# Two-layer graph network on one core: the stage between the layers rewritten, its tables made elsewhere

## The reference, cut to what matters

```python
h = relu(layernorm(x))
# layer 0: an edge network gives a 16x16 matrix per edge
w = (relu(ea16 @ W1 + b1) @ W2 + b2).reshape(E, 16, 16)
out = segment_sum(einsum('ei,eio->eo', h[src], w), dst) + h @ root + bias
out = (out - out.mean(0)) / sqrt(out.var(0) + eps) * gamma + beta      # batch norm
x = x + relu(out)
h = relu(layernorm(x))
# layer 1: tensor product of h[dst] with 8 edge features, summed at src
m = silu(einsum('ei,ej,ijh->eh', h[dst], ea8, W_msg_tp) * c) @ W_msg_lin * c2
agg = segment_sum(m, src)
x = (x + h) + silu(einsum('ni,nh,ihk->nk', h, agg, W_upd_tp) * c3) @ W_upd_lin * c2
```

## Time and profile before

| | us |
|---|---|
| median of 3 runs (lowest, highest) | 7573.94 (7566.49, 7576.72) |
| the profiled execution | 7580.85 |
| its span | 7579.1 |

### The profile page before, as it was taken

How to read it: one execution, slowest core, us unless ns; L and a number is a source line. 1 busy time by engine, 2 the same in 40 slices (tenths; PEclk the granted TensorE clock), 3 DMA queues, 4 the chain that set the end, 5 groups by cost and what they waited for, 6 DMA issues and landing times. The chain is left out here.

```text
span 7579.1 us, 190087 instructions
## 1 busy us (share of the span) xinstructions
PE 6892.4 (91%) x52101; PEld 5979.1 (79%) x52101; DVE 6492.7 (86%) x16891; ACT 4377.7 (58%) x8232; POOL 5712.3 (75%) x4880
## 2 busy tenths in 40 slices
PE   6999999999999999999997699999999999999984
PEld 4777777777777777777776599999999999999981
DVE  6888888888888888888888899999999999999985
ACT  3444444444444444444443577777777777777760
POOL 5777777777777777777776388888888888888880
PEclk9999999999999999999999899999999999999997
DMA  2111111111111111111111454444555555545442
GB/s 53 20 20 20 19 20 20 20 20 20 20 20 20 19 20 20 20 20 20 20 20 33 99 73 73 72 72 71 73 74 71 73 72 72 73 72 74 72 57 39
DMA packets 699525, 333.83 MB, mean 44 GB/s; under 512 B 422354, under 2 KB 643920, under 8 KB 699498
## 3 DMA queue, kind: packets, MB, share of 16 engines
q0 software_dynamic: 336128, 66.50, 15.4%
q1 hardware_dynamic: 362188, 263.59, 13.8%
q10 hardware_dynamic: 1182, 3.44, 0.1%
HBM read 300.69 MB, written 32.35 MB: 44 GB/s over the span
## 5 line engine op out<-in xcount | busy, mean ns | idle before, releaser
L695 POOL DMA_INDIRECT xg<-gather_rows,idx x3232 | 3069.1, 950 | 998.7 <-issue 980.3
L1445 POOL DMA_INDIRECT sums<-total,row x1616 | 2617.9, 1620 | 535.5 <-issue 410.0
L805 PE MATMUL ps_w<-W2s,hT 128*128 128x256 f32 x12928 | 2977.4, 383 | 46.2 <-DVE prod L869 43.4
L805 PEld LDWEIGHTS ps_w<-W2s,hT 128*128 128x128 f32 x12928 | 2431.7, 190 | 562.1 <-DVE prod L869 201.0
L1416 PE MATMUL ps_wide<-hot_col,placed 128*128 128x392 f32 x12928 | 2437.4, 346 | 20.2 <-ACT hot_col L1358 11.4
L1416 PEld LDWEIGHTS ps_wide<-hot_col,placed 128*128 128x128 f32 x12928 | 2317.0, 196 | 51.4 <-issue 39.0
L869 DVE TENSOR_TENSOR prod<-ps_w,xg 128x512 f32<-128x512 f32 x1616 | 1079.6, 689 | 502.3 <-DMA xg<-gather_rows,idx 338.9
L734 ACT ACTIVATE hT<-ps_h,b1c 128x512 f32<-128x512 f32 x1616 | 1018.0, 680 | 312.9 <-PE ps_h L793 312.0
L1257 DVE SCALAR_TENSOR_TENSOR placed<-iota,src_r,halves 128x512 fp32r<-128x512 bf16 x1616 | 1103.1, 744 | 0.1
L1352 ACT ACTIVATE square<-iota_col,minus_col 128x784 bf16<-128x784 int16 x1212 | 1056.4, 934 | 17.0 <-PE ps_wide L1416 17.0
L876 DVE TENSOR_REDUCE msg<-prod 128x32 f32<-128x512 f32 x1616 | 1058.6, 676 | 0.0
(11 more groups left out here) (185 smaller groups left out, 4995.7 us busy)
## 6 DMA issues: line engine op xcount, KB each, us to landing
dst_row<-dst_rows SPq DMA_DIRECT2D x404, 256.0 KB
xg<-gather_rows,idx POOLq DMA_INDIRECT x3232, 2.4
src_row<-src_rows SPq DMA_DIRECT2D x404, 128.0 KB
q_win<-q_rows SPq DMA_DIRECT2D x404, 96.0 KB
ea<-in_edge_attr SPq DMA_DIRECT2D x404, 64.0 KB
sums<-total,row POOLq DMA_INDIRECT x1616, 3.1
e<-in_edge_attr SPq DMA_DIRECT2D x404, 32.0 KB
q_rows<-Q SPq DMA_DIRECT2D x13, 768.0 KB, 3.5
```

The lines of the kernel that those rows point to most:

```text
L695: pool.indirect_dma_start(xg[r][:, t, :], None, k.rows, bass.IndirectOffsetOnAxis(ap=idx[r][:, t:t + 1], axis=0)).then_inc(xg_in[r][t], 16)
L805: last = pe.matmul(bank[:, w, :, :].rearrange("p i o -> p (i o)"), hT[half][:, j, col:col + P], k.W2[:, j, :], start=(j == 0), stop=(j == 1))
L1445: pool.indirect_dma_start(k.sums[t], bass.IndirectOffsetOnAxis(ap=row[s][:, t:t + 1], axis=0), total[s][:, t, :], None, compute_op=ALU.add ...
```

## The change

In `between`, all work on the node tables is done on the 98 real blocks (1568 values) instead of 104, and Q has 100 blocks, 25 pieces (`S.QB`) instead of 26. The multiplications by `valid` over the whole table become one small multiplication of the last block. The squares of both norms move to ACT, in two halves of 49 blocks, each half signalled by itself. Clamp and addition become one DVE instruction, scaling and clamp of the layer norm another. In the Q loop DVE makes the residue and now also the middle part (a copy from fp32 to bf16), GpSimd makes the low part by a subtraction, and ACT only the high part; there are three residue buffers. GpSimd makes `x + h` after the loop. The loops over the pieces are written out instead of being hardware loops.

The tables of the second layer (`gap`, `src_col`, `minus_col`, `src_r`) are made by DVE in `layer0`, after the edge parts of the first three tiles and before the first tile's products; `iota_col` and the clearing of `acc_wide` are done by GpSimd at the start of `between`, the copy of `base_t` by DVE there. The two small blocks at the start of `layer1` are gone. In `layer1` the `dst_row` load is issued first, before the wait for `l1_tables`, and the two small copies of the weight column come between `set_windows` and `node_id`.

```diff
@@ layer0, DVE, after edges_lo(2)
+                v.tensor_scalar(k.gap[:, :, :], k.src[:, :, 0:TP], k.trash[:, 0:1], None, ALU.subtract)
+                link(v.tensor_copy(src_i[:, :, :], k.src[:, :, TP:]))
+                link(v.tensor_scalar(src_i[:, :, :], src_i[:, :, :], int(math.log2(HI)), None,
+                                     ALU.arith_shift_right))
+                link(v.tensor_copy(k.src_col[:, :, :], src_i[:, :, :]))
+                v.tensor_scalar_mul(k.minus_col[:, :, :], k.src_col[:, :, :], -1.0)
+                link(v.scalar_tensor_tensor(k.src_r[:, :, :], k.src_col[:, :, :], float(-HI),
+                                            k.src[:, :, TP:], ALU.mult, ALU.add))
@@ between, GpSimd
+        pool.memset(k.acc_wide[:, :, :], 0.0).then_inc(n["iota_set"], 1)
+        pool.iota(k.iota_col[:, :], pattern=[[1, 2 * S.LC]], base=0, channel_multiplier=0
+                  ).then_inc(n["iota_set"], 1)
+        for piece in range(NP4):
+            b0 = 4 * piece
+            pool.wait_ge(n["q_mid"], piece + 1)
+            pool.tensor_tensor(k.Q[:, b0:b0 + 4, 2, :], res[piece % 3][:, :, :], k.Q[:, b0:b0 + 4, 1, :],
+                               ALU.subtract).then_inc(n["q_lo"], 1)
+        pool.tensor_tensor(k.x[:, 0:B, :], k.x[:, 0:B, :], k.h[:, 0:B, :], ALU.add).then_inc(n["x_added"], 1)
+        pool.wait_ge(n["x_added"], 1)
@@ between, DVE
-        link(v.tensor_tensor(t0[:, :, :], agg, valid, ALU.mult))
-        v.tensor_reduce(sums[:, :], t0[:, :, :].rearrange("p b f -> p f b"), X, ALU.add).then_inc(n["bn_part"], 1)
+        blank_rest()
+        v.tensor_reduce(sums[:, 0, :], agg.rearrange("p b f -> p f b"), X, ALU.add).then_inc(n["bn_part"], 1)
+        v.tensor_copy(k.base[:, :], k.first_node[:, :])
...
-        link(v.tensor_tensor(agg, agg, over(mean), ALU.subtract))
-        link(v.tensor_tensor(agg, agg, valid, ALU.mult))
-        link(v.tensor_tensor(t0[:, :, :], agg, agg, ALU.mult))
-        v.tensor_reduce(sums[:, :], t0[:, :, :].rearrange("p b f -> p f b"), X, ALU.add).then_inc(n["bn_part"], 1)
+        for b0, b1 in HALVES:
+            part = k.agg[:, b0:b1, :]
+            link(v.tensor_tensor(part, part, over(mean, b0, b1), ALU.subtract))
+            if b1 == B:
+                blank_rest()
+            v.sem_inc(n["bn_centred"], 1)
+        for i, (b0, b1) in enumerate(HALVES):
+            v.wait_ge(n["bn_squared"], i + 1)
+            v.tensor_reduce(sums[:, 1 + i, :], sq[:, b0:b1, :].rearrange("p b f -> p f b"), X, ALU.add
+                            ).then_inc(n["bn_part"], 1)
...
-        link(v.tensor_scalar_max(agg, agg, 0.0))
-        link(v.tensor_tensor(k.x[:, :, :], k.x[:, :, :], agg, ALU.add))
-        norm.vector(v, link, k.x, k.h)
+        link(v.scalar_tensor_tensor(x, agg, 0.0, x, ALU.max, ALU.add))
+        link(v.tensor_reduce(lmean[:, :], x, X, ALU.add))
+        link(v.tensor_scalar_mul(lmean[:, :], lmean[:, :], 1.0 / D))
+        for b0, b1 in HALVES:
+            v.tensor_tensor(k.h[:, b0:b1, :], k.x[:, b0:b1, :], over_f(lmean, b0, b1), ALU.subtract
+                            ).then_inc(n["ln_centred"], 1)
+        for i, (b0, b1) in enumerate(HALVES):
+            v.wait_ge(n["ln_squared"], i + 1)
+            link(v.tensor_reduce(lvar[:, b0:b1], sq[:, b0:b1, :], X, ALU.add))
...
+        for b0, b1 in HALVES:
+            part = k.h[:, b0:b1, :]
+            v.scalar_tensor_tensor(part, part, 0.0, over_f(lsd, b0, b1), ALU.max, ALU.mult
+                                   ).then_inc(n["h1_ready"], 1)
+        def mid(piece):
+            v.wait_ge(lin.taken, piece + 1)
+            v.tensor_copy(k.Q[:, 4 * piece:4 * piece + 4, 1, :], res[piece % 3][:, :, :]
+                          ).then_inc(n["q_mid"], 1)
+        for piece in range(NP4):
+            b0 = 4 * piece
+            v.wait_ge(n["q_hi"], piece + 1)
+            need(v, n["q_lo"], piece - 2)
+            y = lin.bank((piece // 2) % 2, piece % 2)[:, :].rearrange("p (b w) -> p b w", w=P)
+            v.tensor_tensor(res[piece % 3][:, :, :], y, k.Q[:, b0:b0 + 4, 0, :], ALU.subtract
+                            ).then_inc(lin.taken, 1)
+            if piece >= 1:
+                mid(piece - 1)
+        mid(NP4 - 1)
@@ between, ACT, after the turned weights (bd_turned)
+        for i, (b0, b1) in enumerate(HALVES):
+            a.wait_ge(n["bn_centred"], i + 1)
+            a.activation(sq[:, b0:b1, :], k.agg[:, b0:b1, :], ACT.Square).then_inc(n["bn_squared"], 1)
@@ layer1, SP
-                sp.wait_ge(q["l1_tables"], 1)
...
+                    sp.dma_start(dst_row[s][:, :],
+                                 k.dst_rows[bass.ds(g, 1), :].broadcast_to([P, GE])
+                                 ).then_inc(in_sems["drow_in"][s], 16)
+                    if isinstance(g, int) and g == 0:
+                        sp.wait_ge(q["l1_tables"], 1)
```

More of the change, by code:

```diff
@@ L566, with __init__ @@
 class NodeLinear:
-    def __init__(self, nc, S, sem, c, name, src, weights, width):
+    def __init__(self, nc, S, sem, c, name, src, weights, width, last=None):
+        self.last = last
         self.S, self.k_src, self.weights, self.width = S, src, weights, width
@@ L595, in product @@
             for j in range(self.pieces):
+                if self.last is not None and c * self.pieces + j >= self.last:
+                    continue
                 need(pe, self.taken, c * self.pieces + j + 1 - self.ring)
@@ L626, in _, with set_windows @@
         v.wait_ge(done, 1)
-def set_windows(v, link, k, last, step):
+def set_windows(v, link, k, last, step, last_row):
     link(v.tensor_scalar_min(k.win[:, :], k.base[:, :], float(last)))
-    v.tensor_copy(k.win_i[:, :], k.win[0:1, :])
+    v.tensor_scalar_min(k.win_i[:, :], k.win[0:1, :], float(last_row))
     link(v.tensor_scalar_add(k.base[:, :], k.base[:, :], float(step)))
@@ L985, in _ @@
                 sp.dma_start(t[D * b:D * (b + 1), b, :], w).then_inc(n["bdf_in"], 16)
-        for c_ in range(S.NC):
-            sp.wait_ge(n["q_lo"], 2 * (c_ + 1))
-            rows = k.q_rows[c_ * T * P:(c_ + 1) * T * P, :]
-            sp.dma_start(rows.rearrange("(b p) f -> p b f", p=P),
-                         k.Q[:, c_ * T:(c_ + 1) * T, :, :].rearrange("p b a w -> p b (a w)")
+        for b0 in range(0, S.QB, T):
+            b1 = min(b0 + T, S.QB)
+            sp.wait_ge(n["q_lo"], b1 // 4)
+            sp.dma_start(k.q_rows[b0 * P:b1 * P, :].rearrange("(b p) f -> p b f", p=P),
+                         k.Q[:, b0:b1, :, :].rearrange("p b a w -> p b (a w)")
                          ).then_inc(n["q_stored"], 16)
@@ L1038, in _ @@
-        each(v, S.NC, body, head=2 + S.NC % 2)
+        link(v.tensor_tensor(agg, agg, over(var, 0, B), ALU.mult))
+        link(v.tensor_tensor(agg, agg, over(k.beta, 0, B), ALU.add))
+        link(v.scalar_tensor_tensor(x, agg, 0.0, x, ALU.max, ALU.add))
[4 more added lines that the diff above has]
+                            ).then_inc(n["ln_centred"], 1)
@@ L1045, in _ @@
                      ACT.Copy).then_inc(n["bd_turned"], 1)
+        for i, (b0, b1) in enumerate(HALVES):
+            a.wait_ge(n["bn_centred"], i + 1)
+            a.activation(sq[:, b0:b1, :], k.agg[:, b0:b1, :], ACT.Square).then_inc(n["bn_squared"], 1)
         a.wait_ge(n["bn_var"], 1)
         a.activation(mean[:, :], var[:, :], ACT.Sqrt).then_inc(n["bn_sd"], 1)
-        norm.scalar(a)
-        def parts(c_, s, use):
-            if not isinstance(c_, int) or c_ + 1 < S.NC:
-                lin.copy(a, c_ + 1, 1 - s)
-            for j in range(2):
-                piece, b0 = c_ * 2 + j, c_ * T + 4 * j
-                a.wait_ge(lin.done, piece + 1)
-                y = lin.bank(s, j)[:, :].rearrange("p (b w) -> p b w", w=P)
-                a.activation(k.Q[:, bass.ds(b0, 4), 0, :], y, ACT.Copy).then_inc(n["q_hi"], 1)
-            for j in range(2):
-                piece, b0 = c_ * 2 + j, c_ * T + 4 * j
-                a.wait_ge(lin.taken, piece + 1)
-                a.activation(k.Q[:, bass.ds(b0, 4), 1, :], res[j][:, :, :], ACT.Copy).then_inc(n["q_mid"], 1)
@@ L1062, in _ @@
-        lin.copy(a, 0, 0)
-        each(a, S.NC, parts, head=3 - S.NC % 2, tail=1)
+        for i, (b0, b1) in enumerate(HALVES):
+            a.wait_ge(n["ln_centred"], i + 1)
+            if i == 0:
+                a.wait_ge(n["bn_part"], 3)
+            a.activation(sq[:, b0:b1, :], k.h[:, b0:b1, :], ACT.Square).then_inc(n["ln_squared"], 1)
+        a.wait_ge(n["ln_var"], 1)
+        a.activation(lsd[:, :], lvar[:, :], ACT.Sqrt).then_inc(n["ln_sd"], 1)
+        lin.copy(a, 0, 0)
+        for piece in range(NP4):
+            ch, j, b0 = piece // 2, piece % 2, 4 * piece
+            if j == 0 and ch + 1 < S.NC:
+                lin.copy(a, ch + 1, (ch + 1) % 2)
+            a.wait_ge(lin.done, piece + 1)
+            a.activation(k.Q[:, b0:b0 + 4, 0, :],
+                         lin.bank(ch % 2, j)[:, :].rearrange("p (b w) -> p b w", w=P),
+                         ACT.Copy).then_inc(n["q_hi"], 1)
```

(16 more changed lines are left out.)

101 lines of the change are left out of this document (36 added, 65 removed).

## The result

| | us |
|---|---|
| before, median of 6 runs (lowest, highest) | 7568.56 (7562.07, 7576.72) |
| after, median of 6 runs (lowest, highest) | 7695.15 (7691.54, 7699.33) |
| ratio, 95% interval | 1.0166 (1.0153 to 1.0179) |
| the profiled execution of after, its span | 7691.54, 7689.8 |

What follows compares the result with a forecast made beforehand. Both layers were taken to run at GpSimd's pace. The terms, -7.05 + 3.6 - 10.1 - 2.8 + 3.2 = -13.2 us, took the median from 7573.94 to 7560.7 us, with a range of 7541 to 7579.

Steps and rivals of the forecast that it cites:

- Layer 1's start: First tiles of layer 1: dst_row issued first brings the first product 1.9 us sooner, 2.8 us gained in all (1 to 3.5).
- Later tiles have the load well ahead: Layer 1 behind its third tile: dst_row comes early enough anyway, so no gain or loss was counted there.
- Rival 3: Layer 1: the share of 113 us in stretched scatters shifts by a tenth, 11 us either way, 7549 or 7572; chance 0.18.
- Norms: Between the layers, DVE's start to PE's first transpose: three parts gain 2.5, 1.35 and 3.2, together 7.05 us (4.5 to 9.5).
- The new wait behind the turned weights: First norm: ACT's squares queue behind the turned weights, ending at 4159.66; that part's gain is 2.5 us, 5.0 if the DMA landed in time.
- Q loop: Between the layers: GpSimd's subtraction (1.25) and DVE's cast take turns, 1.61 us a round; stage loses 3.6 us.
- Rival 1: Q loop: GpSimd and DVE do not hinder each other, the loop gains 4.6 us, total 7552 or 7549; chance 0.21.
- rival 2: Q loop: a subtraction costs 2.04 us, the round 2.40, the loop loses 23.7 us, total 7581; chance 0.09.
- Blocks taken out: Start of layer 1: from the base_t copy to the loop block's first instruction, 10.14 us go.
- Tables in layer 0: Start of layer 0: four gathers beside DVE's table operations lose 0.5 to 1.6 us each, 3.2 us in sum (0.5 to 6).

Runs made afterwards that it cites:

- a_hold: After, its load order kept, but SP begins a tile's loads only once ACT is past its wait for a scatter's landing; 1.0006 of before, scatter pitch 1.927 us.

## Why the prediction was wrong

**Layer 1's start, the step that failed.** The term itself held: first product 7.34 us behind the block's start (7.35 forecast, 9.26 before), `same` late by `src_row`. The failure is the sentence "Later tiles have the load well ahead". It priced the move at nothing in all tiles behind the third because nobody waits for `dst_row`. It didn't ask who has packets on the way when 256 KB are issued earlier. What the runs showed in its place is 111 us: the scatters' mean rose from 1.62 to 1.69, and the old order alone brings the kernel back to 1.0004. The trace of before had the answer in reach: ACT waits for the landing 393 times, 694 us, the row shown above, which I hadn't used. Rival 3 had the right quantity, the 113 us of stretched scatters, and was set aside with "Nothing in the change touches this"; it doubled them instead, ten times the 11 us that I had allowed.

**Norms.** -7.05 forecast, -7.14 measured (35.45 to 28.31 us, start to PE's first transpose): 15.16 to 12.53, 7.79 to 6.43, 12.50 to 9.35 against gains of 2.5, 1.35 and 3.2. The new wait behind the turned weights is there: the first square starts as they end, and the first reduction waited 1.52 us for it.

**Q loop.** The mechanism was right, cast and subtraction take turns; the size a little high: subtraction 1.16 (1.25), round 1.52 (1.61), stage +1.4 (+3.6). Rival 1 falls with the casts of 0.99, rival 2 with the subtraction of 1.16. Moving the work back, with all else of the change kept, gains 6.1 us in the stage (48.64 to 42.49), so the move is a loss, as forecast, and a larger one than the +1.4 against before shows: the other edits of the loop hid most of it. The price of the Trainium skill (GPSIMD Engine Reference, section 3.1, Elementwise), an estimate of 1.12 us here, was nearer than mine: the trace has 1.16.

**Blocks taken out.** 10.1, as forecast: the loop block now comes straight behind the barrier.

**Tables in layer 0.** Four gathers were stretched, here two of them, beside DVE's six operations:

```profile
101.49 1.05 DVE L934 TENSOR_SCALAR gap<-src_t,trash 128x1616 f32<-128x1616 f32 x1
```

```profile
101.74 1.84 POOL L706 DMA_INDIRECT xg<-gather_rows,idx  x1 [0.30 <-issue]
103.88 1.77 POOL L706 DMA_INDIRECT xg<-gather_rows,idx  x1 [0.30 <-issue]
```

Together 2.7 us (3.2 forecast). But layer 0 ended 17.4 later, not about 3: some 13 us are the longer gathers, for which no term and no rival stood. This is the second miss, and it is as large as the whole gain that was forecast.

**The sum without the order.** Between the layers -15.5 was forecast for the stretch that is -17.8, counted from DVE's first instruction there. With the order put right alone, after is at 1.0004, not at 0.998: the gathers take the gain back.

## What to carry to other kernels

A load that is moved ahead has two prices: who waits for it, and whose transfers it now lies in front of. Look for each wait of the form "engine <- DMA" in the steady state, however far from the load, and place the large loads just behind that landing, by a wait if need be, so that the landing they make late is one that nobody waits for: the same order of loads cost 1.6% without it and nothing that can be told with it. Before an edit is priced at nothing because it touches only queues that are ahead, ask what sets the rhythm of the engine that is the bound; and to take a wait away it isn't enough to give it another buffer or another counter, if what it then waits for is the same event one step on.

## What the runs showed of the hardware

- GpSimd's own time for a scatter of 128 rows (1.55 us) that starts beside DVE's `placed` operation is mostly longer by what is left of that operation, to within 0.15 us; where it finds no gap it lasts until `hot_col` behind the block has ended and then takes its 1.55 (3.17 in all).
- A scatter's landing, 3.0 to 3.1 us behind its start, becomes 3.8 when a 256 KB load of SP's is issued in the first 1.5 us (after, fourth scatter, 175 tiles), and 4.7 with another 128 KB right behind it (before, first scatter, 320 tiles). Issued 0.2 to 0.5 us ahead of the start it makes 4.5 (a_hold, second scatter). A 32 KB load leaves it at 3.0.
- A GpSimd increment that stands ahead of a scatter is seen more than two scatters early: the count of the second scatter of a tile released ACT 0.6 us ahead of the start of the last one of the tile before.
- GpSimd instructions between the layers go with gathers that are about 6 ns longer in the layer before them; unexplained.
- GpSimd's fp32 subtraction of 512 values takes 1.16 us, its addition of 1568 values 3.48, 2.2 ns a value.
- DVE's cast of 512 values takes 0.42 us alone and 0.97 to 1.00 beside such a subtraction.
